# Second attention layer: the value product by 32-row blocks of each batch, in two rounds over four banks

## The reference

```python
# second layer, first half (B = 32 batches, T = 32 tokens, H = 16 heads, DH = 128)
ada = (timestep_embed @ ada_w + ada_b)[:, None, :]
shift1, scale1, gate1, shift2, scale2, gate2 = jnp.split(ada, 6, axis=-1)
x1 = _ln(x) * (1.0 + scale1) + shift1
qkv = (x1 @ qkv_w + qkv_b).reshape(Bc, Tc, 3, H, DH)
q, k, v = (qkv[:, :, 0], qkv[:, :, 1], qkv[:, :, 2])
attn = jnp.einsum('bthd,bshd->bhts', q, k) * DH ** (-0.5)
attn = jax.nn.softmax(attn, axis=-1)
attn_out = jnp.einsum('bhts,bshd->bthd', attn, v).reshape(Bc, Tc, INNER)
attn_out = attn_out @ out_w + out_b
x = x + gate1 * attn_out
```

## Time and profile before

| | us |
|---|---|
| median of 3 runs | 670.09 |
| lowest and highest | 668.68, 670.34 |
| profiled execution | 665.65 |
| its span, first to last instruction | 663.70 |

### The profile page before, as it was taken

One profiled execution on the slowest core, in us unless ns is written; L12 is line 12 of the kernel. 1 busy time (PEld: TensorE's weight loads), 2 busy tenths in 40 slices (PEclk: granted clock), 3 DMA queues, 4 the chain that ended last, 5 costly groups with the idle time before them and its releaser, 6 DMA issues.

```text
span 663.7 us, 13680 instructions
## 1 busy us (share of the span) xinstructions
PE 617.6 (93%) x5642; PEld 519.5 (78%) x5642; DVE 385.3 (58%) x689; ACT 329.1 (50%) x836; POOL 191.2 (29%) x194
## 2 busy tenths in 40 slices
PE   3688999999999899998999999999999998789997
PEld 1567888888888688887877888888788887668776
DVE  3689778877777736755674254162342527852553
ACT  2577668776682335433346454554445343355440
POOL 0664434324341405522135040140120003632000
PEclk9789999999999799999999999999999999989999
DMA  8450000000000554535001030120000002100023
GB/s 280 169 191 2 1 2 1 3 2 2 1 1 3 198 140 124 175 112 179 5 1 37 30 96 1 33 66 1 1 2 0 2 1 65 33 5 28 1 66 126
DMA packets 12607, 36.28 MB, mean 55 GB/s; under 512 B 2153, under 2 KB 3689, under 8 KB 11937
## 3 DMA queue, kind: packets, MB, share of 16 engines
q1 hardware_dynamic: 12304, 34.36, 16.2%
q10 hardware_dynamic: 240, 1.05, 0.6%
HBM read 34.29 MB, written 1.11 MB: 53 GB/s over the span
## 4 chain that ended last, share of the span: by engine, by line
PE 77%; DVE 10%; ACT 5%; DMA 2%; issue 2%; POOL 1%; SPq 0%; DVEq 0%; ACTq 0%
PE ps L1312 18%; PE ps L1313 17%; PE ps L1314 17%; PE ps L1436 8%; PE ps L1606 4%; PE ps L1389 2%; PE ps L1764 2%; DMA xT<-in_x_T 2%; ACT hid L623 1%; PE ps L1419 1%; PE ps L1594 1%; PE ps L1407 1%; DVE strm_lo L1179 1%; PE ps L1341 1%; ACT strm_hi L791 1%
## 5 line engine op out<-in xcount | busy, mean ns | idle before, releaser
L1179 DVE SCALAR_TENSOR_TENSOR strm_lo<-ps,col,strm_hi 128x512 fp32r<-128x512 f32 x32 | 24.0, 751 | 113.4 <-ACT strm_hi L791 112.1
L477 POOL TENSOR_TENSOR w_lo<-raw_w,w_hi 128x1024 fp32r<-128x1024 f32 x20 | 49.4, 2485 | 132.1 <-ACT w_hi L591 110.8
L1312 PE MATMUL ps<-w_hi,act_hi 128*128 128x512 f32 x160 | 65.8, 412 | 6.0 <-ACT junk L584 3.3
L775 ACT ACTIVATE work<-ps,col 128x512 f32<-128x512 f32 x64 | 44.2, 690 | 49.1 <-PE ps L1314 49.0
L1312 PE MATMUL ps<-act_hi,w_hi 128*128 128x512 f32 x160 | 63.0, 394 | 1.8 <-POOL act_lo L539 1.2
L1313 PE MATMUL ps<-w_lo,act_hi 128*128 128x512 f32 x160 | 63.9, 399 | 0.0
L1314 PE MATMUL ps<-w_hi,act_lo 128*128 128x512 f32 x160 | 63.7, 398 | 0.0
L1314 PE MATMUL ps<-act_hi,w_lo 128*128 128x512 f32 x160 | 62.4, 390 | 0.0
L1313 PE MATMUL ps<-act_lo,w_hi 128*128 128x512 f32 x160 | 62.3, 389 | 0.0
L1436 PE MATMUL ps<-raw_w,raw_s 128*128 128x256 f32 x256 | 61.5, 380 | 0.3 <-ACT raw_s L677 0.3
L1436 PEld LDWEIGHTS ps<-raw_w,raw_s 128*128 128x128 f32 x256 | 46.2, 190 | 5.8 <-ACT raw_s L677 0.5
(11 more groups left out here) (189 smaller groups left out, 1471.0 us busy)
## 6 DMA issues: line engine op xcount, KB each, us to landing
raw_w<-in_w_attn SPq DMA_DIRECT2D x16, 512.0 KB, 4.4
raw_s<-in_w_moe SPq DMA_DIRECT2D x11, 384.0 KB, 4.4
work<-comb_dram SPq DMA_DIRECT2D x10, 256.0 KB, 4.0
work<-comb_dram SPq DMA_DIRECT2D x18, 128.0 KB, 2.9
raw_w<-in_w_qkv SPq DMA_DIRECT2D x4, 512.0 KB, 12.4
raw_w<-in_w_o SPq DMA_DIRECT2D x1, 2048.0 KB, 7.8
raw_s<-in_w_ffn SPq DMA_DIRECT2D x8, 256.0 KB, 2.8
bd<-in_w_ada SPq DMA_DIRECT2D x1, 1536.0 KB, 6.5
```

Source lines behind the costliest of these rows:

```text
L477: G.tensor_tensor(flat(w_lo[:, slot]), raw, flat(f32(w_hi[:, slot])), ALU.subtract).then_inc(s_piece_lo, 1)
L775: A(dst[:, h * BANK:(h + 1) * BANK], src, ACT.Identity, bias=c_(b, 4 * j + h)).then_inc(s_q1_copied, 1)
L1179: V.scalar_tensor_tensor(flat(strm_lo[:, n % SS]), ps[:, 4 + n % 2, :], c_("bv", 4 * (u // CHUNKS) + h), flat(f32(strm_hi[:, n % SS])), AL ...
L1312: mm(dst, ah, bh, start=start and i == 0, stop=False, **flags)
```

## The change

- **Value product.** `pv1(u, turn)` does all four heads in two rounds. A round has 32 products. Each takes the 32 rows of one batch: weights `v1` (32 rows by 128 features), and 32 streamed columns of `pT` (that batch's probabilities, transposed). In each group of four products the batches 0 to 3 of a tile go to four different banks, 2 to 5: the bank is chosen by the parity of the head and the parity of the batch. The second round does the other half, with heads exchanged between batch pairs, and waits for the first.
- **Place.** The two rounds of unit u - 1 stand inside `proj1(u)`, ahead of groups k = 10 and k = 11. The four output heads follow the scores directly. In the last round both rounds stand behind the warming transposes.
- **Banks.** Scores go to bank 0, so `proj1(u)` waits at k = 0 until the scores of the unit before have been subtracted, and `scores1` waits for the copy of group k = 10. `turn_x2(0)` waits for the last low part.
- **Softmax.** The four 32x512 transposes into `bd` become one of 128x512 into `pT`. The memset of `bd` goes.
- **Order of tokens.** A head's output lies with the even batches in one bank and the odd batches in the other, so the 512 columns of each half keep this order through `out1` and the sum. `gated` reads `xT` in the same order, and `ada` for gate 1 is written in it by two added small operations on VectorE.
- **ScalarE.** The high parts of heads 0 and 1 come ahead of the copy of group k = 11; those of heads 2 and 3 stay behind the Exp and wait for the low part of the head two before.

```diff
@@ ScalarE
                     n = 12 * u + k
+                    if k == 11 and u >= 1:
+                        take_pv1(u - 1, (0, 1))
                     act.wait_ge(s_proj1, n + 1)
...
             def take_pv1(u, heads):
                 for h in heads:
                     n = 4 * u + h
-                    act.wait_ge(s_pv1, n + 1)
+                    act.wait_ge(s_pv1, 2 * (u + 1))
                     if n >= SS:
                         act.wait_ge(s_out1, n - SS + 1)
 
-                    A(flat(strm_hi[:, n % SS]), ps[:, 4 + n % 2, :], ACT.Identity,
-                      bias=c_("bv", 4 * (u // CHUNKS) + h)).then_inc(s_pv1_hi, 1)
+                    if h >= 2:
+                        act.wait_ge(s_pv1_lo, n - 1)
+                    src, hi, _ = heads_out(u, h)
+                    A(hi, src, ACT.Identity, bias=c_("bv", 4 * (u // CHUNKS) + h)).then_inc(s_pv1_hi, 1)
...
                 if u < U:
                     take_proj1(u)
-                if u >= 1:
+                if u == U:
                     take_pv1(u - 1, (0, 1))
@@ GpSimd
-                if t == 0:
-                    pool.wait_ge(s_ada_mm, 1)
-                    G.memset(bd[:], 0.0).then_inc(s_bd_zero, 1)
@@ VectorE
                 softmax_ratio(s_e1, u + 1)
-                if u >= 2:
-                    dve.wait_ge(s_pv1, 4 * (u - 1))
-                for b in range(BT):
-                    rows = slice(SEQ * b, SEQ * (b + 1))
-                    V.transpose(bd[rows, u % 2, :, b, :], sm_e[rows]).then_inc(s_bd1, 1)
+                if u >= 1:
+                    dve.wait_ge(s_pv1, 2 * u)
+                V.transpose(flat(pT[:]), flat(sm_e[:])).then_inc(s_bd1, 1)
...
+                    for m in range(DK):
+                        n = 2 * DK + m
+                        src = ps[:, 4, n * BATCH:(n + 1) * BATCH].rearrange("p (c a i) -> p c i a", c=CHUNKS, i=2)
+                        dst = ada[:, n, :].rearrange("p (c i a) -> p c i a", c=CHUNKS, i=2)
+                        ins = V.tensor_scalar(dst, src, c_("adab", n), None, ALU.add)
+                    ins.then_inc(s_ada_ready, 1)
@@ TensorE
+                    if k >= 10 and u >= 1:
+                        pv1(u - 1, k - 10)
...
+                    if k == 0 and u >= 1:
+                        pe.wait_ge(s_s1_shifted, u)
...
             def scores1(u):
-                pe.wait_ge(s_q1_copied, 12 * u + 8)
-                if u >= 1:
-                    pe.wait_ge(s_s1_shifted, u)
+                pe.wait_ge(s_q1_copied, 12 * u + 11)
...
-            def pv1(u, h):
-                n = 4 * u + h
-                if h == 0:
+            def pv1(u, turn):
+
+                if turn == 1:
+                    pe.wait_ge(s_pv1, 2 * u + 1)
+                else:
...
                     pe.wait_ge(s_q1_copied, 12 * (u + 1))
-                    pe.wait_ge(s_bd1, BT * (u + 1))
-                if n >= 2:
-                    pe.wait_ge(s_pv1_lo, n - 1)
-                for t in range(CT):
-                    last = mm(ps[:, 4 + n % 2, t * P:(t + 1) * P], v1[:, u % 2, t, h * DH:(h + 1) * DH],
-                              bd[:, u % 2, 4 * h + t].rearrange("p b q -> p (b q)"), start=True, stop=True)
+                    pe.wait_ge(s_bd1, u + 1)
+                    if u >= 1:
+                        pe.wait_ge(s_pv1_lo, 4 * u)
+                for pair in range(2):
+                    for t in range(CT):
+                        for b in range(BT):
+                            odd_head = (b // 2 + turn) % 2
+                            h = 2 * pair + odd_head
+                            rows = slice(SEQ * b, SEQ * (b + 1))
+                            at = pair * D + t * 2 * SEQ + (b // 2) * SEQ
+                            last = mm(ps[:, 2 + 2 * odd_head + b % 2, at:at + SEQ],
+                                      v1[rows, u % 2, t, h * DH:(h + 1) * DH], pT[rows, 4 * h + t, :],
+                                      start=True, stop=True)
                 last.then_inc(s_pv1, 1)
...
                 if u >= 1:
-                    out1(u - 1, 0)
-                    pv1(u - 1, 2)
-                    out1(u - 1, 1)
-                    pv1(u - 1, 3)
-                    out1(u - 1, 2)
-                    if u == U:
-                        pe.wait_ge(s_s1_shifted, U)
-                        turn_x2(0)
-                    out1(u - 1, 3)
+                    for h in range(4):
+                        if u == U and h == 3:
+                            pe.wait_ge(s_s1_shifted, U)
+                            pe.wait_ge(s_pv1_lo, 4 * U)
+                            turn_x2(0)
+                        out1(u - 1, h)
```

More of the change, by code:

```diff
@@ L369, in build_program, with heads_out @@
         Y_BANK = 3
+        def heads_out(u, h):
+            n = 4 * u + h
+            at = (h // 2) * D
+            src = ps[:, 2 + 2 * (h % 2):4 + 2 * (h % 2), at:at + D]
+            hi, lo = (flat(w[:, n % SS]).rearrange("p (i n) -> p i n", i=2) for w in (strm_hi, strm_lo))
+            return src, hi, lo
         def piece_free(i):
@@ L1029, in _ @@
                     dve.wait_ge(s_ada_mm, 1)
-                    V.tensor_tensor(ada[:], ps[:, 4, 0:NADA * BATCH].rearrange("p (n b) -> p n b", n=NADA),
-                                    over(c_("adab", 0, NADA), BATCH), ALU.add).then_inc(s_ada_ready, 1)
+                    link(V.tensor_tensor(ada[:], ps[:, 4, 0:NADA * BATCH].rearrange("p (n b) -> p n b", n=NADA),
+                                         over(c_("adab", 0, NADA), BATCH), ALU.add))
+                    for m in range(DK):
[4 more added lines that the diff above has]
+                    ins.then_inc(s_ada_ready, 1)
                     dve.wait_ge(s_ada_ready, 1)
@@ L1178, in low_heads @@
                     dve.wait_ge(s_pv1_hi, n + 1)
-                    V.scalar_tensor_tensor(flat(strm_lo[:, n % SS]), ps[:, 4 + n % 2, :], c_("bv", 4 * (u // CHUNKS) + h),
-                                           flat(f32(strm_hi[:, n % SS])), ALU.add, ALU.subtract).then_inc(s_pv1_lo, 1)
+                    src, hi, lo = heads_out(u, h)
+                    V.scalar_tensor_tensor(lo, src, c_("bv", 4 * (u // CHUNKS) + h), f32(hi), ALU.add,
+                                           ALU.subtract).then_inc(s_pv1_lo, 1)
             def add_out(u):
@@ L1191, in add_out, with halved @@
                     ins.then_inc(s_acc1, 1)
+            def halved(ap):
+                return ap.rearrange("p (a i q) -> p i a q", i=2, q=SEQ)
             def gated(acc, gate, bias, c, m):
@@ L1197, in gated @@
                                             over(ada[:, gate * DK + m, CB * c:CB * (c + 1)], SEQ), ALU.add, ALU.mult))
+                if gate == 2:
+                    part = yT[:, m, s].rearrange("p (i a q) -> p i a q", i=2, q=SEQ)
+                    return V.tensor_tensor(halved(xT[:, m, s]), halved(xT[:, m, s]), part, ALU.add)
                 return V.tensor_tensor(xT[:, m, s], xT[:, m, s], yT[:, m, s], ALU.add)
@@ L1593, in scores1 @@
                             k = 4 * h + t
-                            last = mm(ps[b * SEQ:(b + 1) * SEQ, 2, k * SEQ:(k + 1) * SEQ], qT1[:, q:q + SEQ],
+                            last = mm(ps[b * SEQ:(b + 1) * SEQ, 0, k * SEQ:(k + 1) * SEQ], qT1[:, q:q + SEQ],
                                       kT1[:, q:q + SEQ], start=True, stop=True)
                 last.then_inc(s_s1, 1)
-            def pv1(u, h):
-                n = 4 * u + h
-                if h == 0:
-                    pe.wait_ge(s_q1_copied, 12 * (u + 1))
-                    pe.wait_ge(s_bd1, BT * (u + 1))
-                if n >= 2:
-                    pe.wait_ge(s_pv1_lo, n - 1)
-                for t in range(CT):
-                    last = mm(ps[:, 4 + n % 2, t * P:(t + 1) * P], v1[:, u % 2, t, h * DH:(h + 1) * DH],
-                              bd[:, u % 2, 4 * h + t].rearrange("p b q -> p (b q)"), start=True, stop=True)
+            def pv1(u, turn):
+                if turn == 1:
+                    pe.wait_ge(s_pv1, 2 * u + 1)
+                else:
+                    if u == 0:
+                        pe.wait_ge(s_xn1_ready, TILES)
+                        pe.wait_ge(s_xT1_copied, TILES)
+                        pe.wait_ge(s_x1_ready, 4)
+                    pe.wait_ge(s_q1_copied, 12 * (u + 1))
+                    pe.wait_ge(s_bd1, u + 1)
[11 more added lines that the diff above has]
+                                      start=True, stop=True)
                 last.then_inc(s_pv1, 1)
```

13 lines of the change are left out of this document (2 added, 11 removed).

## The result

The changed kernel is slower: 679.2 us (median of 4 runs, 674.5 to 681.7) against 669.4 us (median of 4, 667.9 to 670.3), a ratio of 1.014 with a 95% interval of 1.008 to 1.020. The forecast was 680.9, between 674.5 and 688.5. The profiled execution has a span of 675.7 us, 12.0 more than before. Executions differ by some microseconds at the start, where TensorE's granted clock differs too: between 9 and 41 us of the span it is 0.82 of full speed before and 0.73 after, and the first scores of the first layer start at 53.10 and 54.82 us.

A forecast was written before the change was run, and what follows sets the result against it. TensorE, busy 93% of the span, was taken as the bound. Terms 4.8 + 4.55 + 0.95 + 1.5 - 1.0 gave +10.8 us, from the median 670.09 to 680.9 us; 674.5 to 688.5 should hold 8 times in 10.

The forecast's parts named there:

- Value product: Second attention on TensorE: row-block groups take 0.11 us, paced by weight loads; loss 0.69 a unit, +4.8 us over seven.
- Wait before head 2: TensorE stalls before the third output head, old stall before head 3 goes; net +0.65 a unit, +4.55 us over seven.
- Hand-over: After the first unit, the next projection waits for the subtraction of the scores in bank 0; +0.95 us.
- Tail: Last unit: both rounds in the open behind warming transposes, result's transposes wait for head 3's low part; +1.5 us.
- VectorE's relief: Four transposes a unit become one on VectorE, beneath output, projection and warming work; costed at nothing.
- Start: Without the memset, VectorE's small scalings shorten and TensorE's wait for the low part goes; -1.0 us.
- (a): Rival: row blocks paced by their 32 streamed columns, weight loads hidden, a group 0.03 us; 660.6 us; chance 8%.
- (b): Rival: row-block loads and streams run one after the other, 0.98 us more on each of eight units; 688.7 us; chance 10%.
- (c): Rival: the wait before the third output head doesn't come, 7 x 1.10 us less; 673.2 us; chance 10%.
- (d): Rival: no difference, small product loss paid for by the start and VectorE's relief; 668 to 672 us; chance 6%.

The follow-up runs named there:

- place_only: Changed kernel's place, score bank and ScalarE order, but the full-matrix products of the kernel before, memset late; ratio 1.009 to the kernel before.
- stream64: Changed kernel with 64 instead of 32 streamed columns in each row-block product; ratio 1.013 to the kernel before.
- weights64: Changed kernel with 64 instead of 128 weight columns in each row-block product; ratio 0.999 to the kernel before.
- early2_bank6: Changed kernel with head 2 copied ahead of the Exp and the first unit's scores in bank 6 instead of 0; ratio 1.009 to the kernel before.
- memset_late: Kernel before with the memset of bd moved from near the beginning to four pieces between slices of the expert weights; ratio 0.998 to the kernel before.
- heads23: Kernel before with late memset and head 3's value product directly behind head 2's; 664.2 us against 668.4, ratio 0.992.
- early2: Changed kernel with head 2's high and low parts ahead of the softmax's Exp, maximum and subtraction in units 1 to 7; ratio 1.011 to the kernel before.
- memset_back: Changed kernel with the memset of the unused buffer bd put back at its old place on GpSimd; ratio 1.021 to the kernel before.

## Why the prediction held

The sum was 10.8 us and the medians differ by 9.8; within the traces the stretch of the second attention grew by 10.8, against 11.8 for its four terms, and the start gave 1.35 back. The mechanisms are the predicted ones. That the sum is so close is partly luck, because its errors go both ways: the wait was taken 1.7 us too large, the last round's own part 0.4 too large and the gain at the start 0.35 too small, while a slower clock in the last round, which was not foreseen, added about 1.0, and the hand-over 0.2.

- **Value product, +0.69 a unit.** Measured 0.68, from `place_only`. Its step, that 32 streamed columns don't shorten a group, is shown by `stream64` and `weights64`. The last digit is luck: a round costs 2.12 us and not 2.18, and the scores, which now stand behind a pass and no longer behind a product, cost 0.09 on going in (409.00 to 409.32), which the sum left out. The sign named for it, 2.1 to 2.2 us from start to start with the pass behind, was 1.92; the number given counted in the steps on both sides.
- **Wait before head 2, net +0.65 a unit.** The mechanism is right, the term too large: the pass starts 0.77 us late and the one behind it costs 0.11, less the 0.45 that went, 0.4, or 2.8 us in seven units instead of 4.55. I had added up listed durations in a row. In the trace the copy starts 0.54 us after the Exp starts, and VectorE's maximum 0.11 us after the first output pass (410.66 and 410.55) where the kernel before has 0.27.
- **Hand-over, +0.95.** Measured 1.15, since TensorE took up work 0.26 us after the end of the subtraction (359.19 + 0.69 = 359.88, 360.14) and not 0.06. `early2_bank6`, without this wait, got it back.
- **Tail, +1.5.** Measured 2.1, from the first warming transpose to the transposes of the result (13.98 us, 11.88 before). The path is not the predicted one: TensorE and not the low part of head 3 came last.

TensorE in the last round of the changed kernel, timeline, and then the row of the stretch of its passes, with the granted clock as the third figure from the end:

```profile
559.03 2.56 PE L1370 MATMUL ps<-cst 128*128 128x128 f32 x22
561.53 4.06 PE L1637 MATMUL ps<-pT,work 32*128 32x32 f32 x128
567.18 0.67 PE L1329 MATMUL ps<-strm_hi,w_hi 128*128 128x512 f32 x1 [1.59 <-DVE strm_lo L1191]
567.65 0.63 PE L1330 MATMUL ps<-strm_lo,w_hi 128*128 128x512 f32 x1
...
573.01 0.60 PE L1667 MATMUL ps<-cst,xT 128*128 128x128 f32 x4
```

```profile
567.20:571.00 3.80, 3.80 (x10) 2.99 (x11) 3.73 (x6) 1.38 (x2) 0.00 (x0) 0.55 0.00 0
```

After both rounds in the open and an idle of 1.59 us the clock was down to half, passes stood 0.43 us apart, and the low part of head 3, done at 571.87, waited for TensorE instead of the other way round. `place_only` has the same idle, but behind full products. Its timeline of TensorE there, and the row of the same 3.8 us:

```profile
562.96 0.50 PE L1315 MATMUL ps<-strm_hi,w_hi 128*128 128x512 f32 x1 [1.56 <-DVE strm_lo L1182]
...
567.76 0.63 PE L1644 MATMUL ps<-cst,xT 128*128 128x128 f32 x4 [0.38 <-DVE strm_lo L1182]
```

```profile
562.96:566.76 3.80, 3.80 (x17) 3.10 (x18) 3.73 (x6) 1.38 (x2) 0.00 (x0) 1.00 0.01 2
```

Passes stood 0.23 us apart, the low part of head 3 came last as predicted, and the transposes started 12.56 us after the warming ones. The kept traces say that this is no chance of one execution. Granted clock in the 3.8 us from the first output pass of the last round on:

| what multiplies | kernels | granted clock |
|---|---|---|
| full products | before, `memset_late`, `heads23`, `place_only` | 1.00 in each |
| row blocks, 128 weight columns | after, `stream64`, `early2`, `early2_bank6`, `memset_back` | 0.55, 0.58, 0.50, 0.50, 0.50 |
| row blocks, 64 weight columns | `weights64` | 0.66 |

The clock fell behind the row blocks in six traces of six, and behind full products in none of four, of which one has the same idle. How the rounds bring this about is not shown. Of the 1.42 us between 13.98 and 12.56, 0.39 lie ahead of the first output pass, so the clock cost about 1.0 us. Without it the tail would have been some 1.1 us longer than before, where 1.5 had been worked out. So in these traces the row blocks have a second price, on the passes behind them.

VectorE's relief was costed at nothing, as its four transposes were said to lie beneath the warming block. They didn't quite: they held the product up in the kernel before (the rows under `heads23`), where it starts 3.15 us after the warming block and in the changed kernel 2.50. The sum has this all the same, since it counts from the start of the warming block.

- **Start, -1.0.** 1.35 between before and after within the traces (the scores of the first and the second tile start 21.86 and 20.51 us apart). The two scalings took 0.42 us together where some 0.1 had been named. In `memset_back` only 0.2 of it came back, and in the total it can't be told, as above.

Of the rivals, (a) and (b) are excluded by the round's 1.92 us (under 1 and 2.6 had been named for them) and by the two widths, (c) by the rows of the wait, (d) by the interval. The rule of the Trainium skill ("TensorEngine Tiling (Array Packing)", Theoretical Speedup) that a contract dimension of 32 gives up to 4x did not come true here: four blocks do run together, but each product brings its own 128 weight columns, and four times as many loads eat the factor. The other rule cited ("TensorE: Matmul & The Clock Gate", LDWEIGHTS), that a load goes by columns whatever its rows, agrees with the load rows of the trace: 187 ns for 32 rows by 128 columns and 188 for 128 rows by 128 columns, 133 for 32 rows by 64 columns, and 109 for 128 rows by 32.

## What to carry to other kernels

Before a product is cut into row blocks, count the weight columns that are loaded, not the numbers that are multiplied: here each small block brought its own 128, and 64 of them cost more than 16 full products (4.24 us against 3.56 in two rounds). And when work is pulled out from between two steps, look at what it covered: here 1.6 us of product had hidden most of the way from the scores through Exp to the copies, in a queue in which the copies stood behind the Exp. The cheap gain was in the order (one call moved, 4.4 us of the stretch; with the late memset 0.8% of the total), not in the multiplications.

## What the runs showed beside it

- Two small operations on VectorE (two of 128x64) took 3.4 us while GpSimd ran a memset, and 0.4 us without it. In `memset_back` two of 128x32 that read PSUM took 0.41 us beside the memset, as they did in the changed kernel without it. A 128x512 multiplication behind the first scores took 2.5 us, in both kernels, where 0.69 is usual.
- Row blocks between full passes cost more than their groups: 0.09 us going in, 0.16 between the last group and the next pass (1.92 less 16 groups of 0.11), 0.11 on that pass. Full products with 128 streamed columns cost only 0.08, on the pass behind.
- The start differs from one execution to the next, and TensorE's granted clock with it: over the ten traces the clock in the first 55 us lies between 0.72 and 0.88, and the first scores of the first layer start between 53.1 and 57.7 us, which is more than single terms here. Within the stretch of the change the distances between the scores of neighbouring units, from the second on, were steady to 0.1 us in nine of the ten traces (not in `weights64`); the last round was not (5.7 to 6.7 us from the first output pass to the transposes in the six traces with the slow clock).
